# Two graph layers on one core: the fp32 products of a half ahead of its mask products, instead of block by block

## What is computed

```python
# layer 0 (the top-350 selection changes nothing as long as no row has over 350 entries)
sim = tanh(adj * adj) * (adj > 0)
x = layernorm(x + relu(sim @ (tanh(x @ W_proj + b_proj) @ W_gcn) + b_gcn))

# layer 1, the second layer
pos = (adj > 0) @ x                  # a product with a mask of ones and zeros
neg = (adj < 0) @ x                  # zero for this adj
node = concat(pos, neg) @ node_weight + node_bias * diag(adj)
edge = (adj @ x) @ edge_weight + edge_bias * diag(adj)
x = layernorm(x + node + edge)
```

## Time and profile before

| | |
|---|---|
| Median of 3 runs | 645.9 us (645.73 to 647.39) |
| The profiled execution's own time | 645.48 us |
| Its span, first to last instruction | 643.7 us |
| TensorE busy | 606.1 us, 94% |
| VectorE busy | 512.4 us, 80% |
| ScalarE busy | 415.0 us, 64% |
| Mean granted TensorE clock | 0.989 of full speed |

### The profile page before, as it was taken

How to read it: one execution, slowest core, us unless ns; L and a number is a source line. 1 busy time by engine, 2 the same in 40 slices (tenths; PEclk the granted TensorE clock), 3 DMA queues, 4 the chain that set the end, 5 groups by cost and what they waited for, 6 DMA issues and landing times.

```text
span 643.7 us, 5717 instructions
## 1 busy us (share of the span) xinstructions
PE 606.1 (94%) x1952; PEld 339.2 (53%) x1952; DVE 512.4 (80%) x759; ACT 415.0 (64%) x293; POOL 186.6 (29%) x79
## 2 busy tenths in 40 slices
PE   6699989898898989899999999999999999999993
PEld 4444434343343434355565565655655655657993
DVE  2676979797979797999679689788697796897845
ACT  2387475758585858445888486594774884865840
POOL 0387595959595959500000000000000000000000
PEclk9899989999999999999999999999999999999997
DMA  9999989899999995012988668498498495684000
GB/s 248 346 344 336 299 207 307 221 308 231 297 247 298 252 286 103 1 55 81 254 241 239 192 187 226 128 254 214 128 247 230 129 254 156 186 226 127 1 17 18
DMA packets 141118, 130.66 MB, mean 203 GB/s; under 512 B 9379, under 2 KB 141094, under 8 KB 141094
## 3 DMA queue, kind: packets, MB, share of 16 engines
q1 hardware_dynamic: 75270, 66.35, 37.7%
q10 hardware_dynamic: 65824, 64.04, 36.4%
HBM read 128.27 MB, written 2.10 MB: 203 GB/s over the span
## 4 chain that ended last, share of the span: by engine, by line
PE 67%; DVE 20%; POOL 6%; DMA 2%; ACT 2%; issue 1%; ACTq 1%; DVEq 0%
PE acc L894 32%; PE acc L885 11%; DVE a_cols L561 10%; PE stage L896 9%; PE stage L895 9%; POOL a_cols L345 5%; DVE to_cols L599 3%; DVE minus_half L591 3%; PE stage L894 2%; DMA a_rows<-in_adj_dram 2%; ACT a_cols L506 2%; PE to_rows L904 1%; DVE bn L582 1%; PE to_rows L905 1%; DVE x_rows L609 1%
## 5 line engine op out<-in xcount | busy, mean ns | idle before, releaser
L561 DVE STREAM_TRANSPOSE a_cols<-a_rows 128x2048 f32<-128x2048 f32 x128 | 294.0, 2305 | 84.5 <-PE stage L896 45.1
L894 PE MATMUL acc<-a_cols,x_rows 128*128 128x512 f32 (+1 forms) x512 | 248.1, 565 | 0.0
L885 PE MATMUL acc<-a_cols,rhs 128*128 128x512 f32 x512 | 226.2, 599 | 16.6 <-ACT a_cols L506 15.9
L895 PE MATMUL stage<-masks,x_hi 128*128 128x512 f32 (+1 forms) x288 | 208.5, 724 | 0.0
L345 POOL TENSOR_TENSOR a_cols<-a_cols 128x1536 f32<-128x1536 f32 x64 | 175.1, 2745 | 87.3 <-DVE a_cols L561 86.7
L885 PEld LDWEIGHTS acc<-a_cols,rhs 128*128 128x128 f32 x512 | 95.8, 191 | 141.3 <-issue 112.2
L506 ACT ACTIVATE a_cols<-a_cols 128x2048 f32<-128x2048 f32 x64 | 122.3, 1911 | 51.5 <-POOL a_cols L345 51.1
L522 ACT ACTIVATE a_rows<-a_rows 128x4096 f32<-128x4096 f32 x32 | 116.0, 3623 | 33.8 <-DVE a_cols L561 19.5
L525 ACT ACTIVATE a_rows<-a_rows 128x4096 f32<-128x4096 f32 x32 | 115.9, 3623 | 1.0
L896 PE MATMUL stage<-masks,x_lo 128*128 128x512 f32 (+1 forms) x288 | 106.7, 370 | 0.0
L894 PEld LDWEIGHTS acc<-a_cols,x_rows 128*128 128x128 f32 x512 | 94.0, 189 | 20.1 <-issue 0.5
(11 more groups left out here) (80 smaller groups left out, 215.6 us busy)
## 6 DMA issues: line engine op xcount, KB each, us to landing
a_rows<-in_adj_dram SPq DMA_DIRECT2D x120, 512.0 KB, 9.0
a_rows<-in_adj_dram ACTq DMA_DIRECT2D x120, 512.0 KB, 10.0
out_dram<-n_rows SPq DMA_DIRECT2D x28, 64.0 KB, 8.4
x_rows<-in_x_dram SPq DMA_DIRECT2D x8, 128.0 KB, 4.1
x_rows<-in_x_dram ACTq DMA_DIRECT2D x8, 128.0 KB, 5.1
diag<-in_adj_dram SPq DMA_DIRECT2D x16, 1.0 KB
out_dram<-n_rows SPq DMA_DIRECT2D x8, 32.0 KB, 1.6
w_pne<-n_L_gnn_node_weight_dram SPq DMA_DIRECT2D x1, 128.0 KB
```

The source lines that it names most:

```text
L561: nc.vector.transpose(half_out(hs), half_in(s, h % HALVES)).then_inc(turned[layer], 1)
L885: last = nc.tensor.matmul(acc[parity][:], rhs[:, b, :], a_cols[:, h % HSLOTS, k, :], start=(b == 0), stop=(b == BLOCKS - 1))
L894: nc.tensor.matmul(sums, x_rows[:, b, :], cols, start=(b == 0), stop=(b == BLOCKS - 1))
L895: nc.tensor.matmul(sums_m, x1_hi[:, b, :], mask, start=(b == 0), stop=False)
```

## The change

The three matmuls of a block are no longer made together. For each half, TensorE first makes the four products with `a_cols` (`with_adj`), and then the eight with `masks` (`with_masks`), of the same shapes and into the same banks. The waits and the count on `half_used` stand where they stood, at the start and the end of the half. In the first chunk the transposes to rows come after the four fp32 products, and ahead of the eight mask products, instead of after the first block's three.

```diff
-            def products(sums, sums_m, b, cols, mask):
-                nc.tensor.matmul(sums, x_rows[:, b, :], cols, start=(b == 0), stop=(b == BLOCKS - 1))
-                nc.tensor.matmul(sums_m, x1_hi[:, b, :], mask, start=(b == 0), stop=False)
-                return nc.tensor.matmul(sums_m, x1_lo[:, b, :], mask, start=False, stop=(b == BLOCKS - 1))
...
+            def with_adj(sums, h, cols):
+                for k in range(HB):
+                    b = h * HB + k
+                    nc.tensor.matmul(sums, x_rows[:, b, :], cols(a_cols[:, h % HSLOTS, k, :]), start=(b == 0),
+                                     stop=(b == BLOCKS - 1))
+
+            def with_masks(sums_m, h, cols):
+                for k in range(HB):
+                    b = h * HB + k
+                    mask = cols(masks[:, h % HSLOTS, k, :])
+                    nc.tensor.matmul(sums_m, x1_hi[:, b, :], mask, start=(b == 0), stop=False)
+                    last = nc.tensor.matmul(sums_m, x1_lo[:, b, :], mask, start=False, stop=(b == BLOCKS - 1))
+                return last
...
-                    for k in range(HB):
-                        last = block_products(0, h, k)
-                        if h == 0 and k == 0:
-                            turn_to_rows(LAST)
-                    last.then_inc(half_used[1], 1)
+                    with_adj(acc[0][:], h, all_rows)
+                    if h == 0:
+                        turn_to_rows(LAST)
+                    with_masks(acc_m[0][:], h, all_rows).then_inc(half_used[1], 1)
...
-                    for k in range(HB):
-                        last = block_products(parity, h, k)
-                    last.then_inc(half_used[1], 1)
+                    with_adj(acc[parity][:], h, all_rows)
+                    with_masks(acc_m[parity][:], h, all_rows).then_inc(half_used[1], 1)
...
+                    with_adj(last_acc[part][:, 0:tiles * P], h, part_rows_of)
+                    return with_masks(last_acc_m[part][:, 0:tiles * P], h, part_rows_of)
```

More of the change, by code:

```diff
@@ L891, in _, with all_rows @@
             chunks(pe, layer0)
-            def products(sums, sums_m, b, cols, mask):
-                nc.tensor.matmul(sums, x_rows[:, b, :], cols, start=(b == 0), stop=(b == BLOCKS - 1))
-                nc.tensor.matmul(sums_m, x1_hi[:, b, :], mask, start=(b == 0), stop=False)
-                return nc.tensor.matmul(sums_m, x1_lo[:, b, :], mask, start=False, stop=(b == BLOCKS - 1))
-            def block_products(parity, h, k):
-                return products(acc[parity][:], acc_m[parity][:], h * HB + k, a_cols[:, h % HSLOTS, k, :],
-                                masks[:, h % HSLOTS, k, :])
+            def with_adj(sums, h, cols):
[10 more added lines that the diff above has]
+                return last
+            def all_rows(cols):
+                return cols
             def weigh(rows, at, tiles):
@@ L961, in half_products, with part_rows_of @@
                     at, tiles = PARTS[part]
[L962 to L966, removed]
+                    def part_rows_of(cols):
+                        return part_of(cols, at, tiles)
+                    with_adj(last_acc[part][:, 0:tiles * P], h, part_rows_of)
+                    return with_masks(last_acc_m[part][:, 0:tiles * P], h, part_rows_of)
                 def part_rows(part):
```

## The result

The changed kernel takes 643.62 us (median of 13 runs), the kernel before 646.1 us in the same series of 13: a ratio of 0.9968, with a 95% interval of 0.9955 to 0.9982. By the ratio it is faster by 0.32%, about 2.1 us (the medians differ by 2.5), just beyond the 0.3% that the prediction called no change. The profiled execution took 643.64 us with a span of 641.8, against 645.48 and 643.7.

A forecast was written before the change was run, and what follows sets the result against it. TensorE's matmul stream was taken to bound the second layer. A half of 5.30 us before and 5.31 after counted as zero change, as did the last chunk, transposes and end, giving 645.8 us; range 640.5 to 648.0.

The forecast's parts named there:

- What bounds the kernel: In the second layer, about 356 us, only TensorE's stream of matmuls sets the time; VectorE waits 45.1 us for it.
- rival 1: Passages between fp32 and fp32r are paid for and grouping saves them: 8.2 us together, 637.7 us; chance 0.22.
- The forecast's mechanism: Reordering the second layer's matmuls changes nothing measurable, since a passage between fp32 and fp32r costs nothing; chance 0.67.
- what the new neighbours cost: Mask products between two of their kind keep the 0.235 us slot of the boundary hi to lo, at 512 columns.
- the comparison of lo with hi: Both slots are 0.235 us though only lo has an fp32 product behind it, so that passage costs under 0.005 us.
- The last paragraph of the prediction: Signs to check; the prediction is wrong if a slot's length depends on what stands two or more places ahead.
- The yardstick: Half an fp32 slot, 0.2145 us; the fp32r slot's 0.0205 us above it estimates what could be saved.
- The argument from the width: The fp32r excess falls from 0.0205 us at 512 columns to 0.0135 at 256: a slower stream, no fixed passage price.
- The long record of hi: hi's 797 ns record, against 592 for fp32, might show a paid passage, but was counted as waiting.
- The formula of the Trainium skill: Columns over 2.4 GHz plus about 2.5 ns gives mask slots of 0.216 us; grouping might then save 7.4 us.
- The moved transposes: In the first chunk they come some 2.1 us later, with 1.9 us of cover left before L621: price zero.
- Rival 2: A run of fp32r cannot keep a pair's pace, losing from the third matmul on: 8.2 us, 654 us; chance 0.11.

## Why the prediction came out as it did

**What bounds the kernel** was right. TensorE's stream is the second layer's time; a nanosecond per slot went to the end undiminished, and VectorE's wait for it fell from 45.1 us to 43.0.

**The time** lies in the range, 643.62 in 640.5 to 648.0, but 2.2 us below the forecast of 645.8. It is there because the range was drawn wide enough to hold half of rival 1; the span of the forecast alone, 644.9 to 647.0, misses it. "Faster by over 0.3%" had a chance of 0.22, and at 0.32% it came true only just. The forecast's mechanism, that a passage costs nothing, was wrong, and rival 1 was right in kind: grouping saves, and it does so by removing passages. Its size was over three times too large: 8.2 us in all, 6.9 at 512 columns, against a measured 2.6, and +1.3 at 256 against -0.2.

**The step that failed** is "what the new neighbours cost". I took the boundary from hi to lo, 0.235 us, as the case of two mask products side by side. It was not: both stand within three slots of an fp32 product, where the slot is 233 to 234 ns, and the settled slot of 227 does not occur at 512 columns in the second layer of before. The term "8 mask slots x 0.235" should have been three of 232 and five of 226.7. For the same reason the comparison of lo with hi proved nothing, and the first fp32 slot behind lo, at 431 ns, was taken for the usual 429. I looked for the price in the slot at the boundary, and it is spread over the slots behind it. The last paragraph of the prediction named this gap, a slot that depends on what stands two or more places ahead, but no term and no chance went with it.

**The yardstick** of rival 1, half an fp32 slot, 0.2145 us, was wrong for fp32r. Of the 0.0205 us above it only some two fifths belong to the passage (16 ns over two slots); the settled fp32r slot keeps 12 ns of it even sixteen in a row, and with no fp32 product around. bf16 in the same place has 215.8 ns.

**The argument from the width** (0.0205 us of excess at 512 columns, 0.0135 at 256, so a slower stream and no fixed price) mixed two things, and read the fp32 slot at 256 columns as 0.213 us where the trace has 0.215. Some 11 to 12 ns are in every fp32r slot at both widths (118 against 107.5 at 256); the passage adds 8 a slot at 512 and nothing, or less, at 256. So the excess isn't a rate, and the price isn't fixed; the sum of both only looked like one.

**The long record of hi.** The prediction saw a 797 ns record and called it waiting. After the change only the first hi of each run has it. In the bf16 version in the order of before it is gone (the groups by form, columns as in the earlier trace rows):

```profile
L895 PE MATMUL stage<-masks,x_hi 128*128 128x512 bf16 x206 | 78.1, 379 | 0.0
```

But at 256 columns hi's record is long too, 469 ns against 280 for lo, and there a round trip costs nothing. So the long record marks the passage from fp32 to fp32r, and says nothing of a price.

**The formula of the Trainium skill** (page "TensorE: Matmul & The Clock Gate", section "Back-to-back issue gap"), which the page gives for a single matmul, makes 0.216 us of 512 columns. That agrees with the trace for bf16, 215.8 ns, and not for fp32r, 226.7 ns when settled. The estimate of 7.4 us made from it was too large for that reason, and because at 256 columns nothing was saved.

**The moved transposes** cost nothing, as predicted: they start at 280.57 us, 2.6 us later, of which 0.5 is the later start of the whole second layer, and VectorE's L621 at 282.98 is only these 0.5 later. **Rival 2**, the run that cannot keep its pace, is refuted: in runs of 8 and 16 the slots from the fourth on are shorter than the first three, not longer.

## What to carry to other kernels

Where TensorE bounds a stage, look at the slots several places behind a change of format, not only at the boundary, and average them over many repetitions. A slot that looks settled because its neighbours are equal may be in a state that never settles in the order at hand. If fp32 and fp32r matmuls must share a stream, put as many of a kind together as the buffers allow, eight or more at 512 columns. Smaller groups gain little here: runs of four saved 13 ns of 5307 a half, runs of eight 47, and at 256 columns grouping lost a little. The whole gain was 0.32% of the time, and bf16 operands gained 1.4%, so the format of the operands deserves the question first, where the accuracy allows it.

## What the runs showed of the hardware

- A matmul of 512 columns with its own weight load has a slot of 226.7 ns in fp32r when settled and of 215.8 ns in bf16; an fp32 instruction has 429 ns.
- In runs of 8 and 16 at 512 columns the first three fp32r slots behind fp32 products are each 5 to 6 ns longer than the rest, whatever VectorE does. In runs of two both are 6 to 8 ns longer, whatever bank they write and whatever tile the fp32 product streams. In a run of four the first three are 8 to 12 ns longer. Behind fp32 products, bf16 slots are not longer at all. The cause within TensorE was not found. That the weight load (188 ns for fp32r, 98 for bf16) sets it is a guess that no run separated from the stream, and at 256 columns slots of 118 ns with the same load speak against a plain bound by it.
- In the first 40 us the granted clock differed between executions of the same code (0.96 or 0.91), and the second layer started between 275.2 and 279.8 us in the runs of this study, by more than the effect under study. Two executions of one kernel started it at 277.7 (0.91) and 275.2 us (0.96), and the second layer behind it took the same time to 1 ns.
